# First keys and queries from the centred input, and a new order of statistics, splits and copies in the first stage

## The reference, cut to what matters

```python
xn = _layernorm(x, axis=-1)
XQ = (xn @ q_w.T) ; XK = (xn @ k_w.T) ; XV = (xn @ v_w.T)       # 512 x 512 weights
target = XV - XK
ttt_lr_eta = sigmoid(einsum('bnkc,hdc->bhnkd', xn, ttt_lr_weight) + ttt_lr_bias) / HD
...
x = x + attention(XQ, XK, XV, eta) + ffn(xn, gate_w, up_w, down_w)
```

## Time and profile before

| | |
|---|---|
| median of three runs | 1996.29 us |
| profiled execution | 1993.3 us |
| its span, first to last instruction | 1991.5 us |
| mean granted clock of PE | 0.986 |
| busy share of PE, DVE, ACT, POOL | 94%, 62%, 49%, 51% |
| first stage, to the last Q job | about 194 us |
| DMA in the whole span | 297.71 MB, 149 GB/s in the mean |

### The profile page before, as it was taken

One profiled execution on the slowest core, in us unless ns is written; L12 is line 12 of the kernel. 1 busy time (PEld: TensorE's weight loads), 2 busy tenths in 40 slices (PEclk: granted clock), 3 DMA queues, 4 the chain that ended last, 5 costly groups with the idle time before them and its releaser, 6 DMA issues. The chain is left out here.

```text
span 1991.5 us, 34782 instructions
## 1 busy us (share of the span) xinstructions
PE 1867.1 (94%) x12632; PEld 1414.6 (71%) x12632; DVE 1233.3 (62%) x2416; ACT 984.8 (49%) x2117; POOL 1023.4 (51%) x894
## 2 busy tenths in 40 slices
PE   5899999998998999799999989999999999999998
PEld 3677777666666666587777766777777777777776
DVE  4663576788888875466354456666666666666663
ACT  3332656566665665545443345545444454444442
POOL 5444567566655654510244257555555555556652
PEclk9899999999999999999999999999999999999999
DMA  7786547336334542322788842222323233322320
GB/s 238 275 308 247 183 162 275 119 107 223 122 111 151 186 128 94 113 68 106 249 273 270 293 156 75 95 103 82 124 96 117 96 106 117 117 85 75 102 97 35
DMA packets 150920, 297.71 MB, mean 149 GB/s; under 512 B 13920, under 2 KB 90976, under 8 KB 144096
## 3 DMA queue, kind: packets, MB, share of 16 engines
q1 hardware_dynamic: 149088, 292.34, 43.1%
q10 hardware_dynamic: 1664, 3.15, 0.5%
HBM read 221.52 MB, written 73.92 MB: 148 GB/s over the span
## 5 line engine op out<-in xcount | busy, mean ns | idle before, releaser
L2031 POOL TENSOR_SCALAR probs<-probs,rsum 128x512 f32<-128x512 f32 x256 | 396.6, 1568 | 246.9 <-DVE rsum L2167 246.9
L2131 ACT ACTIVATE p_tok<-bank 128x512 fp32r<-128x512 f32 x256 | 154.9, 608 | 343.5 <-PE bank L2071 343.4
L2163 DVE TENSOR_REDUCE nmax<-bank 128x1 f32<-128x512 f32 x256 | 158.9, 683 | 95.4 <-PE bank L2063 95.4
L2173 DVE TENSOR_TENSOR p_tok<-bank,p_tok 128x512 fp32r<-128x512 f32 x256 | 173.3, 680 | 15.9 <-ACT p_tok L2131 15.8
L2123 ACT ACTIVATE probs<-bank,nmax 128x512 f32<-128x512 f32 x256 | 173.0, 693 | 3.8 <-DVE nmax L2163 3.8
L1519 POOL TENSOR_TENSOR y_pieces<-y_tok,y_pieces 128x512 fp32r<-128x512 f32 x48 | 64.7, 1362 | 186.0 <-ACT y_pieces L1724 185.9
L60 PE MATMUL bank<-xs,ffn_w 128*128 128x512 f32 x352 | 151.7, 431 | 7.5 <-issue 5.5
L2071 PE MATMUL bank<-ident,probs 128*128 128x128 f32 x1024 | 156.1, 276 | 2.8 <-DVE p_tok L2173 2.8
L2071 PEld LDWEIGHTS bank<-ident,probs 128*128 128x128 f32 x1024 | 121.9, 140 | 50.8 <-issue 27.2
L61 PE MATMUL bank<-xs,ffn_w 128*128 128x512 f32 x352 | 138.8, 394 | 0.0
L62 PE MATMUL bank<-xs,ffn_w 128*128 128x512 f32 x352 | 138.7, 394 | 0.0
(11 more groups left out here) (284 smaller groups left out, 4928.9 us busy)
## 6 DMA issues: line engine op xcount, KB each, us to landing
ffn_w<-ffn_pieces SPq DMA_DIRECT2D x116, 512.0 KB, 3.4
uvo<-uvo_pieces SPq DMA_DIRECT2D x15, 2048.0 KB, 8.8
wq<-wq_pieces SPq DMA_DIRECT2D x16, 1536.0 KB, 6.6
ffn_pieces<-stage SPq DMA_DIRECT2D x30, 512.0 KB, 4.6
xs<-xn_pieces SPq DMA_DIRECT2D x4, 2048.0 KB, 8.7
y_tok<-in_gup SPq DMA_DIRECT2D x32, 256.0 KB, 3.8
wk<-wk_pieces SPq DMA_DIRECT2D x16, 512.0 KB, 3.4
ffn_w<-ffn_pieces SPq DMA_DIRECT2D x16, 384.0 KB, 3.5
```

What stands on the lines that cost most here:

```text
L2031: nc.gpsimd.tensor_scalar(probs[:, u % 8, :], probs[:, u % 8, :], rsum[:, u % 8:u % 8 + 1], None, ALU.mult).then_inc(norm_done, 1)
L2131: nc.scalar.activation(p_tok[:, Q % 2, 0, :, hh * P:(hh + 1) * P], banks[4 + u % 2][:].rearrange("p (k q) -> p k q", k=NBLK), ACT.Copy).th ...
L2163: nc.vector.tensor_reduce(nmax[:, u % 8:u % 8 + 1], banks[u % HG][:], axis=X_AXIS, op=ALU.max, negate=True).then_inc(max_done, 1)
L2173: nc.vector.tensor_tensor(p_tok[:, Q % 2, 1, :, q], banks[4 + u % 2][:].rearrange("p (k q) -> p k q", k=NBLK), p_tok[:, Q % 2, 0, :, q].bi ...
```

## The change

1. **First keys and queries from centred input** (block 0 only). ScalarE and VectorE split `xc` as it stands after centring into `first_hi` and `first_lo`, and the K and Q jobs of block 0 use these. Their results are multiplied by 1/std when VectorE copies them out (`scaled`). So the K jobs of block 0 are copied by VectorE and not by ScalarE. V jobs use the normalized parts as before.
2. **PE's order.** `mean` of the next block stands after the second K job, `var` after the second Q job (each two jobs sooner), the rates' sums after the first K job.
3. **ScalarE's order.** In block 0, root, high parts, squares and root of block 1 stand before the first feed-forward pieces; three pieces of block 0 are split at the start of block 1 and three between its key copies. In blocks 1 and 2 the squares stand before the slot's pieces. The high parts are made by token quarters, each as soon as one V job has read the old quarter; the low parts likewise.
4. **VectorE's order.** The reciprocal is apart from the normalization, and both stand between copies; `scan_constants` moves to block 3.
5. **SP and GpSimd.** Eight weight loads and x of block 1 come before the small constant loads; GpSimd's differences V-K run one piece ahead.

The diff, with indentation taken back by eight and cut to what the text speaks of:

```diff
-    on_act = lambda J: jobs[J][0] == "K"
+    on_act = lambda J: jobs[J][0] == "K" and jobs[J][1] > 0
...
+            for r in range(NRAW, NRAW + NF):
+                load_raw(r)
+            load_x(1)
+            for r in range(NRAW + NF, 2 * NRAW):
+                load_raw(r)
             for dst, src in loads:
                 sp.dma_start(dst, src).then_inc(pc_in, 16)
-            load_x(1)
-            for i in range(NW):
-                for r in raw_of[i]:
-                    load_raw(r + NRAW)
+            for r in range(2 * NRAW, 3 * NRAW):
+                load_raw(r)
...
+            for i in range(2 * NF):
+                low(i)
+            target(2 * NF)
+            for i in range(2 * NF, NW):
+                if i + 1 < NW:
+                    target(i + 1)
                 low(i)
...
+            def project(t, kind, j):
+                J = job_at(t, kind, j)
+                bank = banks[J % 4]
...
+                wh, wl = {"K": (kw_h, kw_l), "Q": (qw_h, qw_l), "V": (vw_h, vw_l)}[kind]
+                c = slice(j * P, (j + 1) * P)
+                centred = t == 0 and kind != "V"
+                if j == 0 and (kind == "K" or t == 0) and not centred:
+                    pe.wait_ge(lo_done, NF * (t + 1))
+                for k in range(NF):
                     if t == 0 and j == 0:
-                        pe.wait_ge(pl_done, NF * ("KQV".index(kind) + 1))
-                    wh, wl = {"K": (kw_h, kw_l), "Q": (qw_h, qw_l), "V": (vw_h, vw_l)}[kind]
-                    c = slice(j * P, (j + 1) * P)
-                    for k in range(NF):
...
-                        if kind == "V":
-                            ins = exact_matmul(nc, bank[:], xs_hi[:, k, c], xs_lo[:, k, c], wh[:, k, :], wl[:, k, :],
...
+                    if kind == "V":
...
             mean(0)
+            project(0, "K", 0)
+            project(0, "K", 1)
             var(0)
+            project(0, "K", 2)
+            project(0, "K", 3)
+            project(0, "Q", 0)
+            mean(1)
+            project(0, "Q", 1)
...
-            for t in range(NTB):
-                if t >= 1:
-                    learning_rate(t)
-                project(t, kinds(t)[0])
-                if t == 0:
-                    learning_rate(t)
-                if t + 1 < NTB:
-                    mean(t + 1)
-                project(t, kinds(t)[1])
-                if t + 1 < NTB:
-                    var(t + 1)
+            rate_parts(0)
+            project(0, "Q", 2)
+            rate_sums(0)
+            project(0, "Q", 3)
+            var(1)
+            for j in range(NF):
+                project(0, "V", j)
+            for t in range(1, NTB):
+                rate_parts(t)
...
+                    project(t, kinds(t)[0], j)
+                    if j == 0:
+                        rate_sums(t)
+                    if j == 1 and t + 1 < NTB:
+                        mean(t + 1)
+                for j in range(NF):
+                    project(t, kinds(t)[1], j)
+                    if j == 1 and t + 1 < NTB:
+                        var(t + 1)
                 if t == NTB - 1:
                     pick_rates()
-                project(t, kinds(t)[2])
+                for j in range(NF):
+                    project(t, kinds(t)[2], j)
...
+                if t == 1:
+                    act.wait_ge(ev_dve, ev_count(job_at(0, "Q", NF - 1)))
...
+            def first_split():
+                for k in range(NF):
+                    act.wait_ge(xc_done, k + 1)
+                    nc.scalar.activation(first_hi[k][:], xc[:, k, :], ACT.Copy).then_inc(fhi_done, 1)
+
             def split_x(t):
+                act.wait_ge(y_done, NF * (t + 1))
                 if t >= 1:
-                    act.wait_ge(job_ready, JT * t)
                     act.wait_ge(xs_out, 32 * t)
-                for k in range(NF):
-                    act.wait_ge(y_done, NF * t + k + 1)
-                    nc.scalar.activation(xs_hi[:, k, :], xc[:, k, :], ACT.Copy).then_inc(hi_done, 1)
+                for j in range(NF):
+                    c = slice(j * P, (j + 1) * P)
+                    if t >= 1:
+                        act.wait_ge(job_ready, job_at(t - 1, "V", j) + 1)
+                    nc.scalar.activation(xs_hi[:, :, c], xc[:, :, c], ACT.Copy).then_inc(hi_done, 1)
 
             for i in range(NF):
                 high(i)
+            first_split()
             squares(0)
-            for i in range(NF, NW - NF):
+            for i in range(NF, 2 * NF):
                 high(i)
             act.wait_ge(ready, 3)
             deviation(0)
-            for t in range(NTB):
+            for i in range(2 * NF, NW - 1):
...
+            split_x(0)
+            high(NW - 1)
+            rates(0)
+            squares(1)
+            deviation(1)
+            splits(0, 0)
+            for t in range(1, NTB):
                 split_x(t)
-                if t >= 1:
-                    rates(t)
-                if t == 0:
-                    for i in range(NW - NF, NW):
-                        high(i)
+                rates(t)
+                if t == 1:
+                    splits(0, 1)
                 for j in range(NF):
+                    if t == 1 and j == 2:
+                        splits(0, 2)
                     act.wait_ge(job_ready, JT * t + j + 1)
                     nc.scalar.activation(k_t[:, j, t * TB:(t + 1) * TB], banks[(JT * t + j) % 4][:], ACT.Copy).then_inc(ev_act, 1)
-                if t == 0:
-                    rates(t)
                 if t == NTB - 1:
                     act.wait_ge(lrt_done, NTB)
                     nc.scalar.activation(lr_raw[:], lr_raw[:], ACT.Sigmoid).then_inc(sig_done, 1)
-                splits(t, 0)
                 if t + 1 < NTB:
                     squares(t + 1)
-                splits(t, 1)
+                splits(t, 0)
+                if t >= 2:
+                    splits(t, 1)
                 if t + 1 < NTB:
                     deviation(t + 1)
+                if t == 1:
+                    splits(t, 1)
                 splits(t, 2)
...
-            def normalize(t):
+            def invert(t):
                 dve.wait_ge(std_done, t + 1)
                 nc.vector.reciprocal(std[:], std[:]).then_inc(rec_done, 1)
                 dve.wait_ge(rec_done, t + 1)
+
+            def normalize(t):
+                if t == 0:
+                    dve.wait_ge(fhi_done, NF)
+                    dve.wait_ge(flo_done, NF)
...
+            def first_low():
+                for k in range(NF):
+                    dve.wait_ge(fhi_done, k + 1)
+                    nc.vector.tensor_tensor(first_lo[k][:], xc[:, k, :], first_hi[k][:].bitcast(F32), ALU.subtract).then_inc(flo_done, 1)
+
+            def split_low(t, j):
+                c = slice(j * P, (j + 1) * P)
+                dve.wait_ge(hi_done, NF * t + j + 1)
+                nc.vector.tensor_tensor(xs_lo[:, :, c], xc[:, :, c], xs_hi[:, :, c].bitcast(F32), ALU.subtract).then_inc(lo_done, 1)
+
+            def scaled(kind, j):
+                J = job_at(0, kind, j)
+                dve.wait_ge(job_ready, J + 1)
+                nc.vector.tensor_tensor((k_t if kind == "K" else q_t)[:, j, 0:TB], banks[J % 4][:], std[:], ALU.mult).then_inc(ev_dve, 1)
+
+            def keep_q(t, j):
+                J = job_at(t, "Q", j)
+                dve.wait_ge(job_ready, J + 1)
+                nc.vector.tensor_copy(q_t[:, j, t * TB:(t + 1) * TB], banks[J % 4][:]).then_inc(ev_dve, 1)
+
+            def keep_v(t, j):
+                J, q = job_at(t, "V", j), NF * t + j
+                dve.wait_ge(job_ready, J + 1)
+                if q >= NCS:
+                    dve.wait_ge(cst_out[q % NCS], 32 * (q // NCS))
+                nc.vector.tensor_tensor(cs[:, q % NCS, :], b_row[:], banks[J % 4][:], ALU.add).then_inc(ev_dve, 1)
+
             sum_x(0)
             center(0)
+            first_low()
             sum_squares(0)
+            sum_x(1)
+            invert(0)
+            for j in range(NF):
+                scaled("K", j)
             normalize(0)
-            for t in range(NTB):
-                if t >= 1:
-                    dve.wait_ge(job_ready, JT * t)
-                    dve.wait_ge(xs_out, 32 * t)
-                for k in range(NF):
-                    dve.wait_ge(hi_done, NF * t + k + 1)
-                    nc.vector.tensor_tensor(xs_lo[:, k, :], xc[:, k, :], xs_hi[:, k, :].bitcast(F32), ALU.subtract).then_inc(lo_done, 1)
-                if t >= 1:
-                    rates(t)
-                if t + 1 < NTB:
-                    sum_x(t + 1)
-                    center(t + 1)
-                    sum_squares(t + 1)
-                if t == 0:
-                    rates(t)
-                for kind in kinds(t)[1:]:
-                    if kind == kinds(t)[2] and t == NTB - 1:
-                        dve.wait_ge(picked, 1)
-                        nc.vector.tensor_copy(lr[:].rearrange("p (m c) x -> p c m x", m=NF),
```

(62 more changed lines are left out.)

45 lines of the change are left out of this document (24 added, 21 removed).

## The result

The changed kernel took **2001.56 us** (median of 7 runs, 1997.49 to 2007.63) against 1994.97 (1992.33 to 1996.84) for the kernel before on the same chip: ratio 1.0039, 95% interval 1.0025 to 1.0054. It is slower, where I had forecast 2 us faster. The profiled execution took 2002.48 us, its span is 2000.7. Two single executions among all the runs here, 2605.00 us of the kernel before and 4612.19 us of x2_ring7, had a far lower granted clock (0.655 and 0.409) and count in no ratio.

What follows compares the result with a forecast made beforehand. PE, busy 94% of the span, was taken as the bound, with time won only at its waits or lower clock. Block terms 14.1 + 1.5 - 6.2 - 6.5 - 1.0 gave 1.9 us won: 1996.3-1.9 = 1994.4 us, range 1985 to 2003.

Steps and rivals of the forecast that it cites:

- Block 0: First stage, block 0: first keys at 14.0 us, 14.1 earlier; keys of block 1 at 61.8, a gain of 15.6.
- the x load and the mean of block 1: Block 1: load of x for block 2 at 64.7, PE waits 4.3 us for the mean, keys of block 2 at 109.
- VectorE beside GpSimd: Low parts on VectorE: 3.2 to 3.9 us for four beside GpSimd, not 1.8 each as by the skill's full rule.
- My estimate by that rule: Low parts at the full blocking rule: some 4 us more, keys of block 1 near 65, 1.3 us lost in sum.
- The pieces: ScalarE in block 1: nine feed-forward pieces split in 16.5 us, done at 101.6, before the high parts of block 2.
- slower: Rival, chance 0.21: pieces step at 2.68 us in blocks 1 and 2, 6.9 us lost, 2003.2; decides from 2.15 a step.
- Block 2: Root behind six pieces: PE waits 1.7 and 1.6 us before V2 and V3; keys of block 3 at 153.9, gain 2.9.
- Block 3: Old content plus the rates' sums (1.0 us): takes 37.7 us and ends at 191.6 instead of 193.5.
- The slow clock: PE restarting at 1.2 GHz after waits: up to 2.7 us a restart, 2.2 charged in blocks 0, 1 and 2.
- The gain stays: Rival, chance 0.31: faster pieces, keys of block 2 at 106.1, end at 183.9, 9.6 us won, 1986.7; x in time, 6 more.
- my own signs: Prediction wrong if x lands before 68, steps are under 2 us, or the first stage ends outside 183 to 199.

Runs made afterwards that it cites:

- x2_ring7: The changed kernel with x of block 2 loaded early and seven instead of three piece buffers in blocks 0 and 1; ratio 0.9983 to the kernel before.
- after_again: The changed kernel run and profiled once more with nothing altered; one run, 1999.47 us.
- constants_late: The changed kernel with GpSimd's multiplications of constants held back until the next block's low parts are made; 1998.68 us, ratio 1.0021 to the kernel before.
- all_four: The changed kernel with early x of block 2, seven piece buffers, root of block 3 first, constants behind low parts; 1982.05 us, ratio 0.9956 to the kernel before.
- x2_early: The changed kernel with x of block 2 loaded ahead of the stores of block 0's feed-forward pieces; ratio 1.0029 to the kernel before.

## Why the prediction was wrong, point by point

- **Block 0 was right.** First keys 14.31 (14.0 forecast), first queries 29.71 (28.7), variance of block 1 at 46.30 after a wait of 2.18 (45.6, wait 3.0), root 47.70 (47.2), fourth piece 53.36 (53.7), keys of block 1 at 62.84 (61.8). The gain at that point was 14.6 us of the 15.6.
- **The step that failed first is the x load and the mean of block 1.** I put the load at 64.7, the end of the sum at 72.5, PE's wait at 4.3 and K3 at 81.0. It was 67.99, 79.9, 8.9 and 88.8, late by 7.8; the mechanism was the one that I had described, its size was wrong. Its parts: pieces five to seven started behind the rates' parts at 61.51 (I had the seventh split by 61; V had run 13.1 us, 46.86 to 59.95, its first matmuls at 1.2 GHz, where after_again took 11.5), and their low parts took 4.12 for three, so the load went out 3.3 us late. Its four issues took 2.8 us, where I had 1.5 although shows 2.82, and VectorE could start at 74.86 (I had 71.1). The three additions took 5.0 us where I had 1.4. The second profile of the same kernel had a load at 66.47, the mean at 77.13 and a wait of 4.9 (shorter by 4.0, in part because its slow first key job brought PE there later). So about 3 us of the lateness belong to the first execution; in the second the mean was still 4.6 us later than forecast. From K3 to the keys of block 2 the forecast held: 27.5 us, where I had 28.0.
- **VectorE beside GpSimd was mis-sized too.** The trace shows 0.69 us for a low part alone and 1.37, 1.18 and 2.82 (for two) beside GpSimd, 5.4 for the four before the keys of block 2; I took 3.9 from a row of four. Normalization before the keys of block 3 took 4.73 instead of 3.6. constants_late took the cost of the low parts away by moving GpSimd's work alone. The Trainium skill (SBUF — State Buffer, Who interferes with whom) says that contention for the ports shared by the two engines is an exclusive lock, and that a VectorE instruction with two SBUF inputs contends with a GpSimd instruction that reads SBUF (that the first to issue keeps the others out for a whole instruction it says of VectorE's two-port modes, and I had applied it to all). These rows agree in kind: beside GpSimd a VectorE instruction that takes 0.64 to 0.69 alone took 1.18 to 1.76. So the full price of 1.8 for each was too high on the mean (1.34 before the keys of block 2), as 0.98 was too low. My estimate by that rule, 1.3 us lost, had the measured sign, but that was luck: it charged some 4 us to the low parts of block 1, which met almost no GpSimd work and took 0.69, 0.69 and 1.29 (and 61.8 and 4 make 65.8, by which 2.1 would be lost, where I wrote 65 and 1.3). What was wrong was to take a mean over four instructions, some of which had met no GpSimd work (its constants ended at 117.7, the low parts at 119.4), as the price of one that meets it.
- **The pieces were right, and so was their bound.** Nine took 92.38 to 109.2, 16.8 us (16.5 forecast), a step of 2.02 us by the prediction's count (16.15 us for eight steps). The rival "slower" asked for 2.68 a step and decided from 2.15 upward. Block 1 stayed under that; in block 2 eight steps took 17.5 us (135.61 to 153.15), 2.19 a step with the root among them. The time came out on its side, a little short of its 2003.2, but mainly through another mechanism than its own.
- **Block 2**: waits of 2.22 and 0.95 us (1.7 and 1.6 forecast), a root at 146.59, 14.6 us after K3's end (14.2 forecast), and the block took 48.1 us instead of 44.9. The difference stands in three stretches: up to K3's end 0.8 more, from there to the start of V2 0.5, and from V2 to the keys of block 3 1.9, through a normalization 1.1 longer and low parts of 1.41, 1.18 and 2.82. V2 at the low clock (1.3) cost nothing here by itself, since V3 then waited for VectorE all the same.
- **Block 3**: 38.6 us (37.7 forecast).
- **The slow clock was costed once per block, as one restart.** It came after waits that I had thought harmless: 2.18 us before the variance, 2.22 before V2, 3.85 and 3.65 before the keys. Over the first 200 us the granted clock was 0.91, against 0.96 before:

```profile
0.00:200.00 200.00, 162.60 (x797) 125.26 (x798) 104.90 (x138) 63.79 (x109) 93.65 (x76) 0.96 0.77 267
```

```profile
0.00:200.00 200.00, 163.48 (x772) 124.54 (x773) 106.43 (x135) 62.99 (x106) 90.82 (x70) 0.91 0.73 251
```

- **"The gain stays"** was the rival with the right picture of the kernel as it could be: it put K(2) at 106.1 and the end at 183.9, and with x in time 6 us earlier, 100.1 and 177.9. all_four reached 100.0 and 177.2, closer than such a sum can be trusted, and needed four edits for it. The rival named faster pieces and x in time, and not that the buffers, the root's place and GpSimd have to be changed for them.
- **The whole**: I had forecast 1.9 us won, and the stage lost 9.4 in its first profile (4.1 in the second). By my own signs I was wrong there: the stage was to end between 183 and 199, and it ended at 202.9 (197.6 in the second). 11.3 us separate them: K(1) 1.0, the rest of block 1 6.2, block 2 3.2, block 3 0.9. Not settled: how much of each is the clock and how much contention, since the low clock came behind waits that contention had made longer.

## What to carry to other kernels

Starting a stage earlier moves the time only if each later block finds its data, its buffers and its engines earlier as well: list, for each block, the wait that stands second behind the one you remove, because two waits in series make each cure look useless alone (1.5 and 1.9 us singly, 14.2 together). Ask of every instruction that is moved what the other engine of a shared port does at its new place, and price it from a row in which it certainly met that work, not from a mean. And try to hold off work without a deadline (the constants' multiplications) for a few microseconds rather than let it run beside the last steps before PE.

## What the runs showed of the hardware

- A VectorE addition of two 128x512 SBUF tiles takes 0.64 to 0.69 us alone and 1.18 to 1.76 beside a stream of GpSimd tensor_tensors, whose instructions grow from 1.25 (4.99 for four, after_again at 78.16) to 1.57 or 1.69 us (6.27 and 6.77 for four). Both sides lose. VectorE's centring, which reads one operand from PSUM, took 2.48 us for four both beside GpSimd (after_again at 79.25) and with GpSimd idle (the changed kernel at 126.54).
- DMA issues on SP grow from 0.33 to 1.58 us when the engines are full (share 1.04), and ScalarE, which waited for that 512 KB store, was released 9.5 us after its issue, against a median landing of 4.6. That the transfers ahead in the queue made it late is argued, not shown by a run of its own.
- One core moved 385 GB/s over 13 us (x2_early, 87 to 100 us). The Trainium skill (DMA: Bandwidth & Descriptors, Where 436 GB/s comes from) puts the HBM side of one core at about 358 GB/s; the loads and stores of this kernel, which runs on one core, went above it, so here that figure was no ceiling over such a stretch.
- A wait of about the same length was followed by 1.2 GHz in one profile and not in another: V of block 0, behind 2.18 us of waiting before the variance in the changed kernel and 2.38 in after_again, took 13.1 and 11.5 us (granted clock 0.51 and 1.00 over 47 to 50 us).
